# Attention masks of a recurrent four-layer network added by matmuls of 64 rows by 64 columns

## The chip, the cores and the metric

The program runs on one core of one Trainium2 chip. The metric is the device time of one execution in microseconds (us). The kernel before has a median of 2973.53 us over three runs. Engines are named as in the profile: PE is TensorE's matmul, PEld its weight load, DVE VectorE, ACT ScalarE, POOL GpSimd, and SPq the queue of SyncE, which issues the DMAs.

## The reference, cut to what matters

Four layers run one after another on 16 sequences ("rows") of 256 tokens and 128 channels. Each layer computes `x = x + s * silu(g)` from the layer norm `xn` of `x`. What matters here is the attention inside them:

```
L0 ffn:  local attention, twice (DEPTH = 2), 8 heads of 64, window 64:
         sim = q @ k^T;  mask = (i < j) | (i > j + 64);  softmax;  @ v
L1 attn: 16 heads of 8, causal, alibi bias;  softmax(att + bias) @ v
L2 attn: 16 heads of 8, causal, rotary, low-rank q, k, v
L3 attn: 16 heads of 8 + 32 rotary, causal, latent k, v
```

The other halves of the layers (a recurrent mixer, feed-forward networks, a mixture of experts, a Fourier filter) are not touched.

## The kernel before, in words

Each attention is one block in which every engine walks through a software pipeline of rows: in step `i` a row is projected, row `i-2` gets its scores and maxima, row `i-3` its exponentials, row `i-4` its values, row `i-5` its output (`rows_pipeline`, with a loop over the middle rows). Inside a step, rounds `x` go over pairs of heads, head e = 0 in rows 0 to 63 of the stacked operands and head e = 1 in rows 64 to 127. There are 4 rounds a row in the local attention (`local_attention`, called for two layers) and 8 in `attention`, which the alibi, the rope8 and the latent attention share. So there are 128 rounds in the local attentions together and 128 in each of the other three.

The scores are made twice. First, `scores` (L1156, local L731) writes q by k of a pair into two PSUM banks, one for each head, `masks` (L1163, local `score_masks`, L736 and L738) adds the mask, and DVE takes the row maxima (L1286 and L1287, local L921 and L922). Later the same scores are made transposed with the maximum subtracted by extra rows: `keyed` (L1175, local L749 and L754) writes into banks 6 and 7, `keyed_masks` (L1181, local L759 and L761) adds the mask, ACT takes the exponential (L1247, local L859), and `values` (L1196, local L774 to L776) multiplies by v. All of these matmuls accumulate into the same banks without clearing them after the first.

A mask is added by a matmul whose weights are the whole 128x128 identity and whose moving operand is a bf16 table: 128 columns of `causal_q` or `causal_k` for each of the two diagonal blocks of a head, or 128 and 192 columns of the local bands for a head. That makes four matmuls for a pair of heads and eight for a round, since the keyed masks and the score masks of a round follow each other. The last of each four signals ACT or DVE.

PE's order in a round of `attention` is: scores(x); keyed and keyed masks of an earlier row; score masks(x); then one of the odd jobs by x (x=0 `turn_back` L1134, x=1 `shifts` L1102, x=2 `output` L1141, x=5 `value_rows` L1114, x=7 `turn` L1125, and the projections `product`: one at x=3 in alibi, two at x=3 and 4 in rope8, five at x=2 to 6 in latent); in even rounds `values` of two pairs. In the local attention it is: scores; keyed; both masks; `columns_of` L718 (four transposes); `product` L709; value projection L782 or turn L794; values; at a row's end `output` L802.

What orders the rounds: `scores` waits until DVE has read the maxima of the bank that it reuses (`deep` is 2 bank pairs in alibi and rope8, 1 in the latent attention), `keyed` waits for the exponential of the round before (one bank pair), `keyed` at x=4 waits for a DMA of the row maxima (L1034), and `scores` at x=0 waits for the stacks of its row, brought by 18 DMAs a row in alibi and rope8 (L1046), which SPq issues behind that one. SPq in turn waits for `at_mt`, DVE's L1292 after `shifts`.

The tables come from `const_cast`, are loaded as f32 into `k.Y` by one DMA (L2136) and cast to bf16 by one DVE instruction (L2155) ahead of the first layer norm.

Of the kernel before, what the change touches and what calls it, by code (L numbers as in the profile page):

```python
# [19 lines left out]
P = 128  # L20
# [18 lines left out]
def const_cast():  # L39

    i = np.arange(P)
    ident = np.eye(P)
    causal = np.where(i[None, :] <= i[:, None], 0.0, BIG)
    band = lambda q, k: np.where((q - k >= 0) & (q - k <= 64), 0.0, BIG)
    q, k, j = i[:, None], i[None, :], np.arange(192)[None, :]
    local_q0 = band(q, k)
    local_q1 = band(q + 128, j + 64)
    local_k0 = band(j, i[:, None])
    sel = np.zeros((P, H8 // 2, P))
    for r in range(0, P, 32):  # L50
        for y in range(H8 // 2):
            sel[r + y, y] = 1.0
    parts = [("ident", ident), ("causal_q", causal), ("causal_k", causal.T), ("local_q0", local_q0),
             ("local_q1", local_q1), ("local_k0", local_k0), ("sel", sel.reshape(P, -1))]
    return parts


def const_f32():
# [76 lines left out]


CAST = widths([(n, a.shape[1]) for n, a in const_cast()])
CONF = widths([(n, a.shape[1]) for n, a in const_f32()])
DH = [d * 1 + h * D8 for d in range(D8) for h in range(H16)]
# [33 lines left out]

class Core:
    pass


def at_least(eng, sem, value):
# [448 lines left out]
def local_attention(k, layer, w, rope, X0, Yd):  # L627

    nc, s, ps = k.nc, k.s, k.ps
# [4 lines left out]
    with ExitStack() as ctx:  # L634
# [66 lines left out]
        def _(pe):  # L701
# [30 lines left out]
                                         start=(cols == 0), stop=False, skip_group_check=True)  # L732

            def score_masks():
                for e in range(2):
                    nc.tensor.matmul(ps[:, 4 + e, 0:P], k.cb("ident"), k.cb("local_q0"), start=False, stop=False,  # L736
                                     skip_group_check=True)
                    m = nc.tensor.matmul(ps[:, 4 + e, P:P + 192], k.cb("ident"), k.cb("local_q1"), start=False, stop=True,  # L738
                                         skip_group_check=True)
                m.then_inc(s.la_score, 1)  # L740

            def keyed(i, n, y):
                if y == 0:
# [11 lines left out]
                                         start=False, stop=False, skip_group_check=True)  # L755

            def keyed_masks():
                for e in range(2):
                    nc.tensor.matmul(ps[:, 6 + e, 0:P], k.cb("ident"), k.cb("local_k0", 0, P), start=False, stop=False,  # L759
                                     skip_group_check=True)  # L760
                    m = nc.tensor.matmul(ps[:, 6 + e, P:P + 192], k.cb("ident"), k.cb("local_k0"), start=False, stop=True,  # L761
                                         skip_group_check=True)
                m.then_inc(s.la_keyed, 1)

            def values(i, n, y):
                u = HP8 * (row0 + i) + y
# [47 lines left out]
            def step(i, n):  # L814
                for x in range(4):
                    row2, row3 = 2 + (x < 1), 3 + (x < 2)
                    if live(i, row2):
                        scores(i - row2, (n - row2) % NS, (x - 1) % 4)
                    if live(i, row3):
                        keyed(i - row3, (n - row3) % NS, (x - 2) % 4)  # L820
                        keyed_masks()
                    if live(i, row2):
                        score_masks()
                    row1 = 1 + (x < 1)
                    if live(i, row1):
                        if x == 1:
                            at_least(pe, s.la_stored, row0 + done(i, 5))
                        if x == 2:
                            at_least(pe, s.la_mt, row0 + done(i, 3))
                        columns_of(i - row1, (x - 1) % 4)  # L830
                    if live(i, 0):
                        product(i, n, x)
                    if live(i, 2) and x in (0, 2):
                        project_values(i, (n - 2) % NS, x // 2)
                    if live(i, 4) and x in (1, 3):
                        turn(i, x // 2)
                    row = 3 + (x < 3)
                    if live(i, row):
                        values(i - row, (n - row) % NS, (x - 3) % 4)
                    if live(i, 5) and x == 0:  # L840
                        output(i)
                    if live(i, 3) and x == 1:
                        shifts(i)
# [141 lines left out]
def attention(k, call, scale, stack_rows, rounds, product_at, value_from, value_w, out_w, out_b, make):  # L985

    nc, s, ps = k.nc, k.s, k.ps
# [3 lines left out]
    with ExitStack() as ctx:  # L991
        sb = lambda n, shape, dt=F32: ctx.enter_context(nc.sbuf_tensor(f"at{call}_{n}", shape, dt))
        a = Core()
# [5 lines left out]
        deep = 2 if split else 1  # L999
# [78 lines left out]
        def _(pe):  # L1078
# [78 lines left out]
                                         start=(cols == 0), stop=False, skip_group_check=True)  # L1157

            def masks(i, n, x):
                for e in range(2):  # L1160
                    o = ps[:, 2 + 2 * (x % deep) + e, :]
                    for cols in (0, 2 * P):
                        m = nc.tensor.matmul(o[:, cols:cols + P], k.cb("ident"), k.cb("causal_q"), start=False,  # L1163
                                             stop=(cols > 0), skip_group_check=True)
                m.then_inc(s.at_score, 1)

            def keyed(i, n, x):
                u = HP * (row0 + i) + x
# [7 lines left out]
                                         start=(cols == 0), stop=False, skip_group_check=True)  # L1176

            def keyed_masks():
                for e in range(2):
                    for cols in (0, 2 * P):  # L1180
                        m = nc.tensor.matmul(ps[:, 6 + e, cols:cols + P], k.cb("ident"), k.cb("causal_k"), start=False,  # L1181
                                             stop=(cols > 0), skip_group_check=True)
                m.then_inc(s.at_keyed, 1)

            def values(i, n, x):
                u = HP * (row0 + i) + x
# [14 lines left out]
            def step(i, n):  # L1201
                for x in range(HP):
                    if live(i, 2):
                        scores(i - 2, (n - 2) % slots, x)
                    row = 3 + (x < KEY_LAG)
                    if live(i, row):
                        keyed(i - row, (n - row) % slots, (x - KEY_LAG) % HP)
                        keyed_masks()
                    if live(i, 2):
                        masks(i - 2, (n - 2) % slots, x)  # L1210
                    if live(i, 5) and x == 0:
                        turn_back(i)
                    if live(i, 3) and x == 1:
                        shifts(i, n)
                    if live(i, 5) and x == 2:
                        output(i)
                    if live(i, 0) and x in product_at:
                        product(i, n, product_at[x])
                    if live(i, VALUE_ROW) and x == 5:
                        value_rows(i, (n - VALUE_ROW) % slots)  # L1220
                    if live(i, 4) and x == 7:
                        turn(i)
                    if x % 2 == 0:
                        row = 3 + (x < VALUE_LAG)
                        if live(i, row):
                            values(i - row, (n - row) % slots, (x - VALUE_LAG) % HP)
                            values(i - row, (n - row) % slots, (x + 1 - VALUE_LAG) % HP)
# [1105 lines left out]
```

## Time and profile before

| | us |
|---|---|
| median of three runs (2969.06 to 2974.83) | 2973.53 |
| the profiled execution's own time | 2965.65 |
| its span | 2963.8 |
| PE busy in it | 2372.4 (80%) |
| DVE busy | 1467.8 (50%) |
| ACT busy | 1140.7 (38%) |
| POOL busy | 637.5 (22%) |

The local attentions take most of the span from about 210 to 650 us and from 770 to 1210 us, the alibi attention 1370 to 1660, rope8 1965 to 2265 and latent 2440 to 2940. A matmul's duration in the profile is its time through the array, not the time that it keeps the next one waiting: read the distance from one start to the next for that. Rows of a timeline merge neighbours of one line: start, time from the first start to the last end, and their count. The start of the last of them is the start plus that time less the mean of one.

### The profile page before, as it was taken

Reading aid. Unit: us, or ns where it says so; the run is one execution under the profiler, and the core shown is the slowest. Engines: PE = TensorE matmul, PEld = TensorE weight load, DVE = VectorE, ACT = ScalarE, POOL = GpSimd, SP = SyncE. Lnnn points to the kernel's source line nnn. Section 1 sums busy time; section 2 is a strip of 40 time slices with the busy share of each in tenths; the row PEclk is TensorE's granted clock in tenths of the full one; section 3 lists DMA queues with packets and bytes.
Section 4 is the critical chain, followed back from the end, with each engine's and each line's share of the span. In section 5 each row is a group of like instructions: output and inputs, shape, how many; then the busy total and the mean of one; then the engine's idle time right before and its main releaser. Section 6 shows DMA issues by size and latency. Waiting matters only on the chain. (4 is left out here: it accounts for less than half of the span.)

```text
span 2963.8 us, 54617 instructions
## 1 busy us (share of the span) xinstructions
PE 2372.4 (80%) x19643; PEld 1552.7 (52%) x19644; DVE 1467.8 (50%) x3082; ACT 1140.7 (38%) x1810; POOL 637.5 (22%) x689
## 2 busy tenths in 40 slices
PE   5487999997799999785888458259997768999987
PEld 1133777773267777332555235135553315777764
DVE  4635666635466664445666123166663254554542
ACT  5623554523254444333555212225453421222223
POOL 0204443300344441011100320521110121211100
PEclk8797999998799999887999789579998867999997
DMA  2000000000000000002222311112220013332320
GB/s 106 0 0 1 1 1 0 0 1 0 0 1 1 0 0 1 1 4 61 76 71 61 144 47 35 46 54 67 72 69 2 32 39 96 99 91 91 91 73 29
DMA packets 81244, 115.93 MB, mean 39 GB/s; under 512 B 10352, under 2 KB 67184, under 8 KB 77720
## 3 DMA queue, kind: packets, MB, share of 16 engines
q1 hardware_dynamic: 79024, 109.35, 12.0%
q0 software_dynamic: 2048, 4.20, 0.5%
q8 instruction: 118, 1.93, 0.3%
q14 instruction: 54, 0.44, 0.0%
HBM read 69.57 MB, written 42.86 MB: 38 GB/s over the span
## 5 line engine op out<-in xcount | busy, mean ns | idle before, releaser
L1247 ACT ACTIVATE at_pr<-ps 128x768 f32<-128x768 f32 x384 | 312.1, 813 | 549.6 <-PE ps L1181 549.6
L1286 DVE TENSOR_REDUCE at_m<-ps 128x2 f32<-128x256 f32 x384 | 163.3, 425 | 424.8 <-PE ps L1163 417.7
L1156 PE MATMUL ps<-at_ks,at_qs 40*128 40x128 f32 (+5 forms) x2048 | 213.6, 308 | 79.4 <-DVE at_m L1287 38.4
L1287 DVE TENSOR_REDUCE at_m<-ps 128x2 f32<-128x512 f32 x384 | 262.1, 682 | 0.0
L692 POOL TENSOR_TENSOR la_tc<-la_ta,la_tb 128x512 f32<-128x512 f32 x128 | 162.3, 1268 | 356.7 <-DVE la_tb L958 356.7
L1175 PE MATMUL ps<-at_qs,at_ks 41*128 41x256 f32 (+5 forms) x2048 | 198.9, 293 | 41.0 <-DMA at_qs<-at_ml 24.1
L709 PE MATMUL ps<-w_l0f,la_hs 128*128 128x512 f32 x256 | 153.8, 686 | 54.9 <-POOL la_hs L674 37.0
L859 ACT ACTIVATE la_pr<-ps 128x640 f32<-128x640 f32 x128 | 90.3, 705 | 267.7 <-PE ps L761 267.4
L1175 PEld LDWEIGHTS ps<-at_qs,at_ks 41*128 41x128 f32 (+2 forms) x2048 | 142.7, 145 | 84.6 <-ACT at_pr L1247 33.5
L1156 PEld LDWEIGHTS ps<-at_ks,at_qs 40*128 40x128 f32 (+2 forms) x2048 | 100.4, 145 | 164.3 <-DVE at_m L1287 66.1
L1196 PE MATMUL ps<-at_pr,at_v 128*32 128x256 f32 (+1 forms) x3072 | 173.3, 337 | 10.5 <-issue 10.1
L956 DVE TENSOR_TENSOR la_ta<-ps,la_tab 128x512 f32<-128x512 f32 x128 | 88.5, 692 | 137.1 <-ACT la_sq L877 137.1
L1181 PE MATMUL ps<-cast 128*128 128x128 bf16 x1536 | 154.8, 224 | 0.0
L1533 POOL TENSOR_TENSOR at_parts<-at_ta,at_tb 128x512 f32<-128x512 f32 x64 | 81.1, 1268 | 341.8 <-DVE at_tb L1523 341.7
L1163 PE MATMUL ps<-cast 128*128 128x128 bf16 x1536 | 153.7, 224 | 0.0
L685 POOL TENSOR_TENSOR la_qn<-la_tc,la_rn 128x512 f32<-128x512 f32 x128 | 133.5, 1043 | 86.4 <-DVE la_rn L945 43.5
L1196 PEld LDWEIGHTS ps<-at_pr,at_v 128*32 128x32 f32 x3072 | 92.1, 110 | 83.5 <-issue 36.2
L1181 PEld LDWEIGHTS ps<-cast 128*128 128x128 bf16 x1536 | 87.9, 98 | 57.0 <-issue 42.5
L774 PE MATMUL ps<-la_v,la_pr 128*128 128x65 f32 x512 | 95.0, 267 | 21.4 <-DVE la_ot L913 21.4
L877 ACT ACTIVATE la_sq<-ps 128x512 f32<-128x512 f32 x128 | 76.7, 599 | 89.6 <-PE ps L709 89.6
L774 PEld LDWEIGHTS ps<-la_v,la_pr 128*128 128x128 f32 x512 | 80.3, 192 | 57.8 <-issue 47.1
L1163 PEld LDWEIGHTS ps<-cast 128*128 128x128 bf16 x1536 | 103.6, 100 | 11.5 <-issue 11.5
(309 smaller groups left out, 5009.7 us busy)
## 6 DMA issues: line engine op xcount, KB each, us to landing
scratch_latent<-at_parts SPq DMA_DIRECT2D x32, 640.0 KB, 4.3
at_qs<-scratch_latent SPq DMA_DIRECT2D x32, 320.0 KB
at_ks<-scratch_latent SPq DMA_DIRECT2D x32, 320.0 KB
scratch_alibi<-at_parts SPq DMA_DIRECT2D x32, 192.0 KB, 2.3
at_ks<-scratch_alibi SPq DMA_DIRECT2D x192, 32.0 KB
scratch_rope<-at_parts SPq DMA_DIRECT2D x32, 192.0 KB, 2.3
at_ks<-scratch_rope SPq DMA_DIRECT2D x192, 32.0 KB
moe_weights<-in_moe SPq DMA_DIRECT2D x1, 4096.0 KB
```

The costliest lines, as they stand in the source:

```text
L685: nc.gpsimd.tensor_tensor(heads(qn[:, x % 2, :]), heads(tc[:, x, :]), rn[:, x, :].unsqueeze(2).to_broadcast([P, H8, D64]), ALU.mult).then_ ...
L692: nc.gpsimd.tensor_tensor(tc[:, x, :], ta[:, x % 2, :], tb[:, x % 2, :], ALU.add).then_inc(s.la_tc, 1)
L709: nc.tensor.matmul(ps[:, 0, :], hs[:, n, t * P:(t + 1) * P], w("wq" if p < 2 else "wk"), start=True, stop=True).then_inc(s.la_product, 1)
L774: nc.tensor.matmul(ps[:, 3, o0:o0 + W65], p[:, P:2 * P], V[:, n, 0, h, :], start=True, stop=True)
L1156: nc.tensor.matmul(o[:, cols:cols + keys], q[:, block_q:block_q + P], kk[:, 0:keys], start=(cols == 0), stop=False, skip_group_check=True)
L1163: m = nc.tensor.matmul(o[:, cols:cols + P], k.cb("ident"), k.cb("causal_q"), start=False, stop=(cols > 0), skip_group_check=True)
L1175: nc.tensor.matmul(ps[:, 6 + e, cols:cols + L - first], kk[:, keys:keys + P], q[:, first:L], start=(cols == 0), stop=False, skip_group_che ...
L1181: m = nc.tensor.matmul(ps[:, 6 + e, cols:cols + P], k.cb("ident"), k.cb("causal_k"), start=False, stop=(cols > 0), skip_group_check=True)
L1196: m = nc.tensor.matmul(o, V[:, n, q, 4 * half + j, 24 * slot:24 * slot + 32], pr[:, x % RING, e, cols:cols + L - first], start=(q == 0 and ...
L1247: nc.scalar.activation(pr[:, p % RING, :, :], ps[:, 6:8, 0:384], ACT.Exp, scale=scale).then_inc(s.at_prob, 1)
L1286: nc.vector.tensor_reduce(m2[:, r, 0, x:16:8], ps[:, m:m + 2, 0:128], AX.X, ALU.max, negate=True)
L1287: nc.vector.tensor_reduce(m2[:, r, 1, x:16:8], ps[:, m:m + 2, 128:384], AX.X, ALU.max, negate=True).then_inc(s.at_max, 1)
```

## The change

The eight whole-array mask matmuls of a round become eight of 64 rows by 64 columns, four for the scores and four for the keyed scores. Each has a 64x64 piece of the identity as weights and moves half of a mask's rows. For head e the two matmuls read table rows 64e to 64e+63: one writes the same half of the partitions, and the other the opposite half, for which a second copy of each table is kept with its halves swapped (`_x`). Each moves all columns of its head at once: 2 x 128 (a stepped output) in `attention`, 320 in the local one. The local tables are joined to 320 columns. The packed constants grow from 1408 to 2432 columns, so the DMA L2136 and the cast L2155 do. The order of the work and all waits stay.

```
-    parts = [("ident", ident), ("causal_q", causal), ("causal_k", causal.T), ("local_q0", local_q0),
-             ("local_q1", local_q1), ("local_k0", local_k0), ("sel", sel.reshape(P, -1))]
-    return parts
+    masks = [("causal_q", causal), ("causal_k", causal.T), ("local_q", np.concatenate([local_q0, local_q1], 1)),
+             ("local_k", np.concatenate([local_k0[:, 0:P], local_k0], 1))]
+    crossed = [(name + "_x", np.roll(a, P // 2, 0)) for name, a in masks]
+    return [("ident", ident)] + masks + crossed + [("sel", sel.reshape(P, -1))]
...
+def mask_pair(k, bank, name, cols, twice=None):
+
+    half = P // 2
+    for crossed in range(2):
+        for e in range(2):
+            r = half * e
+            to = half - r if crossed else r
+            rows = k.cb(name + "_x" if crossed else name)[r:r + half, :]
+            out = k.ps[to:to + half, bank + e, 0:cols]
+            if twice:
+                out = out.rearrange("p (c t) -> p c t", t=P)[:, 0:cols // P:twice, :]
+                rows = rows.unsqueeze(1).to_broadcast([half, out.shape[1], P])
+            m = k.nc.tensor.matmul(out, k.cb("ident", r, half)[r:r + half, :], rows, start=False, stop=True,
+                                   skip_group_check=True)
+    return m
...
             def score_masks():
-                for e in range(2):
-                    nc.tensor.matmul(ps[:, 4 + e, 0:P], k.cb("ident"), k.cb("local_q0"), start=False, stop=False,
-                                     skip_group_check=True)
-                    m = nc.tensor.matmul(ps[:, 4 + e, P:P + 192], k.cb("ident"), k.cb("local_q1"), start=False, stop=True,
-                                         skip_group_check=True)
-                m.then_inc(s.la_score, 1)
+                mask_pair(k, 4, "local_q", 320).then_inc(s.la_score, 1)
...
             def keyed_masks():
-                for e in range(2):
...
+                mask_pair(k, 6, "local_k", 320).then_inc(s.la_keyed, 1)
...
             def masks(i, n, x):
-                for e in range(2):
-                    o = ps[:, 2 + 2 * (x % deep) + e, :]
-                    for cols in (0, 2 * P):
-                        m = nc.tensor.matmul(o[:, cols:cols + P], k.cb("ident"), k.cb("causal_q"), start=False,
-                                             stop=(cols > 0), skip_group_check=True)
-                m.then_inc(s.at_score, 1)
+                mask_pair(k, 2 + 2 * (x % deep), "causal_q", 384, 2).then_inc(s.at_score, 1)
...
             def keyed_masks():
-                for e in range(2):
...
+                mask_pair(k, 6, "causal_k", 384, 2).then_inc(s.at_keyed, 1)
```

## Rows read from the trace of the kernel before

**Rows 1.** Page, part 2: PE's granted clock in 40 slices, in tenths.

```profile
PEclk8797999998799999887999789579998867999997
```

**Rows 2.** Waits of PE, 210 to 660 us, local attention: total us, times, longest.

```profile
PE ps L709 <- POOL la_hs L674: 18.6, 15, 4.5
PE ps L774 <- DVE la_ot L913: 10.7, 14, 2.2
```

**Rows 3.** Waits of PE, 1380 to 1650 us, alibi attention.

```profile
PE ps L1175 <- DMA at_qs<-at_ml: 11.6, 16, 2.4
PE ps L1156 <- DMA at_ks<-scratch_alibi: 5.7, 11, 1.2
```

**Rows 4.** Waits of PE, 1975 to 2255 us, rope8 attention.

```profile
PE ps L1134 <- DVE at_ot L1310: 5.8, 14, 0.7
```

**Rows 5.** Waits of PE, 2455 to 2935 us, latent attention.

```profile
PE ps L1156 <- DVE at_m L1287: 32.4, 54, 1.2
```

**Rows 6.** Timeline of PE, alibi: start, us, engine, line, operation, count.

```profile
1501.57 0.87 PE L1196 MATMUL ps<-at_pr,at_v 128*32 128x256 f32 x16
...
1502.81 0.40 PE L1181 MATMUL ps<-cast 128*128 128x128 bf16 x4
1503.04 0.39 PE L1163 MATMUL ps<-cast 128*128 128x128 bf16 x4
1503.27 0.39 PE L1102 MATMUL ps<-conf,at_m 128*128 128x128 f32 x2
1503.59 0.34 PE L1156 MATMUL ps<-at_ks,at_qs 54*128 54x128 bf16 x4
```

**Rows 7.** Timeline of PE, a local round: first mask, first transpose.

```profile
504.18 0.23 PE L759 MATMUL ps<-cast 128*128 128x128 bf16 x1
...
504.75 0.60 PE L718 MATMUL ps<-conf,la_qn 128*128 128x128 f32 x4
```

**Rows 8.** Groups of PE by form: mean ns of one is the last number.

```profile
L1163 PE MATMUL ps<-cast 128*128 128x128 bf16 x1536 | 153.7, 224 | 0.0
L1156 PE MATMUL ps<-at_ks,at_qs 54*128 54x256 bf16 x256 | 35.7, 275 | 0.0
```

**Rows 9.** Groups of weight loads by form.

```profile
L1181 PEld LDWEIGHTS ps<-cast 128*128 128x128 bf16 x1536 | 87.9, 98 | 57.0 <-issue 42.5
L1196 PEld LDWEIGHTS ps<-at_pr,at_v 128*32 128x32 f32 x3072 | 92.1, 110 | 83.5 <-issue 36.2 <-ACT at_pr L1247 16.9
L718 PEld LDWEIGHTS ps<-conf,la_qn 128*128 128x128 f32 x512 | 59.0, 146 | 15.6 <-issue 15.6
L731 PEld LDWEIGHTS ps<-la_qk 64*128 64x128 f32 x1024 | 67.3, 187 | 30.5 <-issue 21.4 <-DVE la_nm L922 5.0
```

**Rows 10.** Timeline of PE between 502.9 and 503.0 us, local scores.

```profile
502.69 0.49 PE L731 MATMUL ps<-la_qk 64*128 64x128 f32 x4
```

**Rows 11.** Timeline, a local row's first round: PE, ACT and DVE.

```profile
514.84 0.23 PE L759 MATMUL ps<-cast 128*128 128x128 bf16 x1
519.01 0.41 PE L774 MATMUL ps<-la_v,la_pr 128*128 128x65 f32 x2 [0.58 <-DVE la_ot L913]
515.32 0.70 ACT L859 ACTIVATE la_pr<-ps 128x640 f32<-128x640 f32 x1 [2.47 <-PE ps L761]
```

**Rows 12.** Timeline of SPq, alibi: first of the maxima, last of the stacks.

```profile
1505.06 1.36 SPq L1034 DMA_DIRECT2D at_qs<-at_mh  x2
...
1512.47 1.99 SPq L1046 DMA_DIRECT2D at_ks<-scratch_alibi  x6
```

**Rows 13.** Timeline, a latent round: PE and DVE.

```profile
2658.29 0.40 PE L1181 MATMUL ps<-cast 128*128 128x128 bf16 x4
...
2660.02 0.49 PE L1156 MATMUL ps<-at_ks,at_qs 40*128 40x128 f32 x4 [0.20 <-DVE at_m L1287]
2658.95 0.43 DVE L1286 TENSOR_REDUCE at_m<-ps 128x2 f32<-128x256 f32 x1 [3.05 <-PE ps L1163]
```

**Rows 14.** Timeline of DVE at the start: the cast of the tables.

```profile
12.76 0.89 DVE L2155 CAST cast<-y 128x1408 bf16<-128x1408 f32 x1 [11.84 <-DMA y<-in_cast]
```

More of the change, by code:

```diff
@@ L757, in keyed_masks @@
             def keyed_masks():
-                for e in range(2):
[L759 to L763, printed above, removed]
+                mask_pair(k, 6, "local_k", 320).then_inc(s.la_keyed, 1)
             def values(i, n, y):
@@ L1178, in keyed_masks @@
             def keyed_masks():
-                for e in range(2):
[L1180 to L1183, printed above, removed]
+                mask_pair(k, 6, "causal_k", 384, 2).then_inc(s.at_keyed, 1)
             def values(i, n, x):
```

## The prediction

> **What bounds the kernel now.** I read the granted clock first: in the slices that hold the middle of the attentions it is 9 or more tenths of full speed [rows 1], so their matmuls are priced at the 2.4 GHz level. Then I read the waits of PE in each attention, and then its timeline, start to start.
>
> In the local attention PE waits once or twice a row, at the row's first round, for POOL's shifted input and for DVE's division [rows 2]; the other three rounds run without a gap. In alibi it waits 16 times for the DMA of the maxima and 11 times for that of the stacks [rows 3]. These hang together: SPq issues from 1505.06 to 1514.46 us without a pause [rows 12], and scores(0) come only after that. So an alibi row is a fixed 11 us chain of DMAs behind `shifts`, plus the two rounds before it. In rope8 scores(0) do not wait for stacks. There PE waits for DVE's division ahead of `turn_back` [rows 4], which comes behind the maxima of round 7. In the latent attention, with one pair of score banks, scores wait for the maxima of the round before, 54 times in 128 [rows 5].
>
> **The mask block.** Before, eight matmuls take 1502.81 to 1503.27 = 0.46 us in the three attentions [rows 6], and 504.18 to 504.75 = 0.57 in the local one [rows 7]. The step of one of 128 columns is 0.056 (L1181's last starts at 1502.81+0.40-0.22 [rows 6, 8], L1163 at 1503.04).
>
> After, each four lie in four different tiles of the array. No row shows 64x64 tiles, so I bound them. The near row is `values`: 16 matmuls of 32 columns of weights, eight of 256 f32 columns and eight of 128, whose passes in series would take 8 x 0.21 + 8 x 0.105 = 2.5 us (0.105 from L1102's two in 0.39 and L718's four in 0.60). Their starts span only 0.87-0.28 = 0.59 [rows 6]: four tiles stream side by side, though all use the same rows. `scores` show the same for two row halves: four f32 passes in two steps [rows 10]. So I take four at a time: a group costs 2 x 0.055 = 0.11, or 0.135 with 320 columns, plus 0.02 for the staggered starts. The far bound is two at a time, 0.22 and 0.27 (first rival).
>
> The weight load of 64 bf16 columns lies between the 98 ns row of the whole identity and the 146 ns one of a transpose [rows 9]. Only the first of a block is uncovered, for 0 to 0.05 us more than now: 0.02. So a block becomes 2 x 0.11 + 0.02 + 0.03 = 0.27 us, and 0.32 locally: **0.19 and 0.25 less**.
>
> **The change of array shape.** L1102's two passes end their stream at 1503.27 + 0.21 = 1503.48, and L1156, which uses half the rows, starts at 1503.59 [rows 6]: 0.10 for changing the shape. Now scores (64x128) change once, into the masks (128x128), and the transposes and projections behind the masks keep that shape. After, the masks are 64x64, so where work of 128x128 follows there is **one change more**. It also uncovers a weight load: the first two passes of L731 after a change lie 0.49-0.28 = 0.21 apart instead of 0.11 [rows 10], so 0.10 for a load of 187 ns, and in proportion 0.05 for what L718's 146 has above 98 [rows 9]. An f32 load of 192 ns is half covered by a mask today, so it loses 0.05 too. Sum: **0.15 us a round** where such work follows: all local rounds, six of eight in alibi, seven in rope8, eight in latent. Bounds: 0, if 64x128 to 64x64 needs no stop (second rival), and 0.20. Behind a round with `values` or scores next there is a change of shape today too: nothing.
>
> The Trainium skill speaks against this change here ("TensorEngine Tiling (Array Packing)", Key Properties and Restrictions): a change of tiling mode drains the engine, and column tiling gives up the fast weight load. The trace agrees with the first, at 0.10 us; the second is not shown, since no bf16 load of under 128 columns stands in it.
>
> **The sum, stage by stage.** A round that PE sets wins 0.19-0.15 = 0.04 (local 0.25-0.15 = 0.10). A round set by the chain to ACT wins in the first four only: they need 0.10+0.02 to stream and 0.275 through the array [rows 8] instead of 0.40, so 0.08 (local 0.10). A round set by DVE's maxima wins the whole block, 0.19, since its second change of shape lies beside DVE.
> - Local: three rounds x 0.09 (0.24 - 0.15, unrounded) + the first, which hangs on keyed masks (514.84), exponential (515.32), division, values (519.01) [rows 11]: 0.10. That is 0.37 a row x 32 rows = 12 us. The first round's score masks win nothing: POOL's input is late there.
> - Alibi: all that is won from x=2 to 7 ends in the wait for the DMAs. Round 0 wins 0.04 and some 0.3 that PE waited ahead of `turn_back`, since round 7 now comes earlier against the DMAs; round 1 wins 0.08. 0.42 x 14 rows = 6 us.
> - Rope8: round 7 0.19 (DVE, `turn_back`), round 1 0.08, 4 0.04, 5 0.08; rounds 2 and 3 end in the wait for the maxima's DMA, 6 in `values`' wait for ACT, 0 in that for DVE. 0.39 x 15 = 6 us. The stacks had some 0.5 us to spare.
> - Latent: the round shown is 3.25 us, of which masks to DVE 0.66 [rows 13], DVE 1.1. By the timeline four rounds of eight wait long enough to win 0.19, one wins 0.13, and three are set by PE: 0.04 each. 1.0 x 15.5 = 15.5 us.
> - Start: the cast is the last thing ahead of the first layer norm, and waits for its DMA [rows 14]. 1024 columns more: 0.89 x 1024/1408 = 0.65 us on DVE, and the DMA's 704 KB become 1216, at the start's some 400 GB/s of shared queues 1.3 to 2.5 us. Together 2.5 us lost.
>
> 12 + 6 + 6 + 15.5 - 2.5 = 37 us. The profiled execution of 2965.65 (span 2963.8 and 1.85 around it) would be 2928.7. The median lies 7.9 us above it: 2973.5 - 37 = **2936.5 us**.
>
> **Rivals.** *Two at a time (slower).* The two matmuls of a head read the same rows of the array, and the crossed one waits for the direct one. Blocks would then take 0.48 and 0.58, so the 0.15 of each change of shape stands without return. Local 96 rounds x 0.17 = 16 us, latent 48 PE-set rounds x 0.17 + the rest = 10, rope8 3.5, alibi 0.5, start 2.5: 33 slower, **3006 us**. It decides from where the second two start over 0.06 us behind the first two (halfway between a sum of -37 and +33). For it: no row has tiles with shared rows and crossed columns and different row halves at once. Against it: `values`, four tiles on the same rows. The Trainium skill has a rule that would bring this about ("TensorE: Matmul & The Clock Gate", Part 3): a weight load overlaps running matmuls only when its row group differs. By that rule the crossed loads wait for the direct matmuls. The trace disagrees for column tiles, where 16 loads and matmuls span 0.59 us.
>
> *No stop between the two row-tiled shapes (faster).* Each block then starts 0.10 earlier: local 12 more, latent 12, rope8 6, alibi 2.5: 32 more, **2904 us**. For it: the row halves stay. Against it: every other change of columns or rows costs 0.10.
>
> *The waits take it all (no change).* If alibi and rope8 win nothing, the local PE-set rounds nothing (a change of shape at 0.20 and a load at 0.05), and the latent DVE rounds half: 2973.5 + 2.5 - 8 = **2968 us**.
>
> *The clock.* With less in the array, PE's clock could fall to 1.2 GHz in places. 23 of 40 slices are at 9 tenths or more [rows 1], 1704 us; if a twentieth of these, 85 us, ran at half clock with PE streaming two thirds of the time, as the timeline of the alibi rows has it, that costs 85 x 2/3 = 57 us: 2936.5 + 57 = 2993.
>
> **Chances.** Forecast 0.66, two at a time 0.14, no stop 0.10, all taken 0.07, clock 0.03. The forecast's own range is 2915 to 2962, by the bounds of the change of shape and the loads. For 8 in 10 I add the faster rival and leave the slower ones out: 2903 to 2965. About 0.2% is what a measurement of this kernel tells from no change. Faster 0.77 (forecast, no stop, and a little less), same 0.06, slower 0.17.
>
> **What the profile after would show.** Four mask matmuls starting within 0.03 us, the next four 0.11 later, and the block at 0.27 (right) or 0.48 (two at a time). A stop of 0.10 ahead of the first mask and again ahead of L718, L1102 or L1499; without the first, the second rival. In alibi longer waits for both DMAs; in the latent attention rounds of 3.06 instead of 3.25 us. The cast ending near 16 instead of 13.65. The prediction is wrong if the stops around small tiles cost more than 0.20, or if the latent rounds keep their length.

## The result, and the profile after

The change makes the kernel slower: 2985.72 us median of 20 runs (2965.93 to 3000.75) against 2964.91 of 20 runs of the kernel before, a ratio of 1.0068 with a 95% interval of 1.0050 to 1.0087. The forecast was 37 us faster, 2936.5 in a range that ended at 2965. Of the kernel before, three runs had stood at 2973.53 and twenty stand at 2964.91, so 8.6 us of the forecast's 2936.5 were in its base. The profiled execution of the changed kernel is the slowest of its twenty, 3000.75 us (span 2998.9): it shows 35 us of loss where the medians have 21. Ratios compare executions in the fast state; of all those below only one, of the wide masks, was not (3014.97 us).

Nearly every step about the matmuls came out as forecast. A local round of the changed kernel, on PE (start, us, engine, line; L191 is the matmul of `mask_pair`, L767 is what was L754, L736 what was L718), then a window of 0.03 us at the first four, and the weight loads of all eight:

```profile
505.41 0.31 PE L767 MATMUL ps<-la_mt,cast 64*128 64x128 bf16 x4
505.64 0.47 PE L191 MATMUL ps<-cast 64*64 64x320 bf16 x8
506.04 0.65 PE L736 MATMUL ps<-conf,la_qn 128*128 128x128 f32 x4
...
505.64 0.33 PE L191 MATMUL ps<-cast 64*64 64x320 bf16 x4
...
505.64 0.14 PEld L191 LDWEIGHTS ps<-cast 64*64 64x64 bf16 x8
```

The first four mask matmuls lie within 0.33 us from the first start to the last end, and one alone takes 0.309 in the mean, so they start within some 0.02 us: four tiles stream side by side, the crossed ones too. The eight end their stream 0.30 us after the first start (0.47 less 0.30 for the time that the last one's record takes, plus 0.133 for its 320 columns). Then comes a stop of 0.10 until L736. Block and stop together are 0.40 where they were 0.57 [rows 7].

An alibi round and a latent round of the changed kernel, PE and DVE:

```profile
1487.48 0.33 PE L1178 MATMUL ps<-at_qs,at_ks 56*128 56x256 bf16 x4
1487.74 0.41 PE L191 MATMUL ps<-cast 64*64 64x256 bf16 x8
1488.08 0.70 PE L1395 MATMUL ps<-xn,w_l 128*128 x2
...
2659.02 0.82 PE L1178 MATMUL ps<-at_qs,at_ks 41*128 41x256 f32 x8
2659.78 0.41 PE L191 MATMUL ps<-cast 64*64 64x256 bf16 x8
2660.12 0.70 PE L1149 MATMUL ps<-at_oT,w_l 128*128 128x256 f32 x2
```

From the first mask to the next whole-array matmul it is 0.34 us, of which 0.25 is the block and 0.09 the stop; it was 0.46 [rows 6]. The weight-load row (PEld) below tells what a 64-column bf16 load is: 108 ns, between the 98 and the 146 of [rows 9]. The two PE rows are the mask matmuls.

```profile
L191 PEld LDWEIGHTS ps<-cast 64*64 64x64 bf16 x4096 | 80.7, 108 | 97.4 <-issue 69.5
L191 PE MATMUL ps<-cast 64*64 64x256 bf16 x3072 | 181.6, 305 | 0.0
L191 PE MATMUL ps<-cast 64*64 64x320 bf16 x1024 | 61.6, 309 | 0.0
```

What did not come out is the clock. The page's row of the granted clock, after, against [rows 1], and the busy times with the granted clock (the number behind POOL) in the stretch of the latent attention, before and after:

```profile
PEclk8797999999799999877998697679988656997965
...
2440.00:2945.00 505.00, 452.81 (x4611) 337.98 (x4610) 224.01 (x480) 135.62 (x207) 79.21 (x75) 0.93 0.27 81
...
2425.00:2998.00 573.00, 524.03 (x4635) 347.82 (x4634) 238.75 (x500) 142.83 (x216) 80.30 (x76) 0.79 0.25 76
```

The last nine slices, which hold the latent attention, are 6, 5, 6, 9, 9, 7, 9, 6, 5 where they were 8, 6, 7, 9, 9, 9, 9, 9, 7. Since the clock has two levels, 1.2 and 2.4 GHz, a mean of 0.79 over 573 us means 2 x 0.21 x 573 = 241 us at the lower one; before it was 2 x 0.07 x 505 = 71. By the clock records of the two traces, from the first projection of a stage to its last output (us, and in brackets us at 1.2 GHz):

| stage | before | after | difference |
|---|---|---|---|
| local attention 1 | 440.8 (54.6) | 432.3 (50.0) | -8.5 |
| local attention 2 | 437.8 (48.5) | 430.6 (38.1) | -7.2 |
| alibi | 305.6 (35.9) | 306.8 (72.1) | +1.2 |
| rope8 | 319.5 (39.6) | 322.2 (79.9) | +2.7 |
| latent | 525.3 (81.8) | 574.7 (253.9) | +49.4 |
| all between, and the ends | 934.9 (341.9) | 932.2 (334.7) | -2.7 |

The rows of the latent attention show how the two go together. A row is the time from its first scores to the next row's (us, 15 of them, one execution):

```
before  24.9 31.2 28.2 28.6 28.7 28.6 29.9 28.7 28.6 29.9 30.0 28.6 28.7 28.7 26.2
after   30.7 37.2 38.6 27.5 27.6 27.5 29.0 29.0 27.5 29.1 40.9 27.5 27.6 27.6 30.7
```

At the high clock a row is 27.53 instead of 28.59 us, 1.06 shorter, as the forecast's 1.0 said. But the first three rows, the row behind the second turn of the loop and the last one run at the low clock. The loop holds the scores of rows 5 to 13. Of the 172 us more at the low clock, 65 lie ahead of it, 31 in it and 76 behind it. Most of the low clock behind it is one stretch, in which no turn of a loop lies:

```profile
2873.00:2941.00 68.00, 65.89 (x468) 42.89 (x468) 14.69 (x30) 15.11 (x23) 0.00 (x0) 0.50 0.07 19
```

One profile is one execution. But the record has the mean granted clock of each, and twice its distance from 1, times the span, is the time at 1.2 GHz. The twenty executions of the changed kernel have 788 us in the median (730 to 828, the profiled one at the top). The kernel before has 611 to 617 on the three chips of the experiments (579 to 657 over its 68 executions). So the change brings some 175 us more, not the 226 of the two profiles.

### The profile page after: what moved, and what is told of

Read it like the earlier page. It is cut to its first block and busy times, and to the rows that moved or that the text cites. A ratio compares the mean times of both kernels' runs of the same rounds, so it can differ in the third digit from the quotient of the medians.

```text
span 2998.9 us, 54617 instructions
## 1 busy us (share of the span) xinstructions
PE 2406.7 (80%) x19643; PEld 1446.5 (48%) x19644; DVE 1472.5 (49%) x3082; ACT 1141.1 (38%) x1810; POOL 636.5 (21%) x689
## 5 line engine op out<-in xcount | busy, mean ns | idle before, releaser
L1164 PE MATMUL ps<-at_ks,at_qs 40*128 40x128 f32 (+5 forms) x2048 | 237.4, 336 | 71.2 <-DVE at_m L1286 26.1
L1178 PE MATMUL ps<-at_qs,at_ks 41*128 41x256 f32 (+5 forms) x2048 | 220.7, 319 | 38.3 <-DMA at_qs<-at_ml 23.7
L191 PE MATMUL ps<-cast 64*64 64x256 bf16 (+1 forms) x4096 | 243.2, 306 | 0.0
L1195 PE MATMUL ps<-at_pr,at_v 128*32 128x256 f32 (+1 forms) x3072 | 191.6, 365 | 16.0 <-issue 15.5
L1178 PEld LDWEIGHTS ps<-at_qs,at_ks 41*128 41x128 f32 (+2 forms) x2048 | 158.3, 161 | 91.0 <-ACT at_pr L1246 31.6
L1164 PEld LDWEIGHTS ps<-at_ks,at_qs 40*128 40x128 f32 (+2 forms) x2048 | 111.9, 160 | 164.8 <-issue 70.6
L703 POOL TENSOR_TENSOR la_qn<-la_tc,la_rn 128x512 f32<-128x512 f32 x128 | 133.4, 1042 | 83.3 <-DVE la_rn L953 41.4
L191 PEld LDWEIGHTS ps<-cast 64*64 64x64 bf16 x4096 | 80.7, 108 | 97.4 <-issue 69.5
L782 PE MATMUL ps<-la_v,la_pr 128*128 128x65 f32 x512 | 95.0, 267 | 18.9 <-DVE la_ot L921 18.9
L782 PEld LDWEIGHTS ps<-la_v,la_pr 128*128 128x128 f32 x512 | 79.9, 191 | 56.4 <-issue 45.8
L749 PE MATMUL ps<-la_qk 64*128 64x128 f32 (+1 forms) x1024 | 105.7, 325 | 0.3 <-DVE la_nm L930 0.2
L783 PE MATMUL ps<-la_v,la_pr 128*128 128x65 f32 x512 | 99.0, 275 | 0.0
```

What stands on the lines that cost most here:

```text
L191: m = k.nc.tensor.matmul(out, k.cb("ident", r, half)[r:r + half, :], rows, start=False, stop=True, skip_group_check=True)
L703: nc.gpsimd.tensor_tensor(heads(qn[:, x % 2, :]), heads(tc[:, x, :]), rn[:, x, :].unsqueeze(2).to_broadcast([P, H8, D64]), ALU.mult).then_ ...
L749: nc.tensor.matmul(ps[:, 4 + e, cols:cols + hi - lo], q[:, first:first + P], kk[:, lo:hi], start=(cols == 0), stop=False, skip_group_check ...
L782: nc.tensor.matmul(ps[:, 3, o0:o0 + W65], p[:, P:2 * P], V[:, n, 0, h, :], start=True, stop=True)
L1164: nc.tensor.matmul(o[:, cols:cols + keys], q[:, block_q:block_q + P], kk[:, 0:keys], start=(cols == 0), stop=False, skip_group_check=True)
L1178: nc.tensor.matmul(ps[:, 6 + e, cols:cols + L - first], kk[:, keys:keys + P], q[:, first:L], start=(cols == 0), stop=False, skip_group_che ...
```

## The experiments

All of them carry the tables of the changed kernel, the wide masks wider ones; "whole" masks are the four 128x128 matmuls of the kernel before. Lengths and low-clock times are those of the profiled execution, ratios those of all runs against the kernel before on the same chip.

**Small masks in the local attentions alone.**

```
-                mask_pair(k, 2 + 2 * (x % deep), "causal_q", 384, 2).then_inc(s.at_score, 1)
+                mask_whole(k, 2 + 2 * (x % deep), "causal_q", CAUSAL_AT).then_inc(s.at_score, 1)
...
-                mask_pair(k, 6, "causal_k", 384, 2).then_inc(s.at_keyed, 1)
+                mask_whole(k, 6, "causal_k", CAUSAL_AT).then_inc(s.at_keyed, 1)
```

> Small masks in the two local attentions alone; whole-array masks elsewhere. Clock theory (the loss is PE's granted clock in the latent attention, the small masks themselves are quicker): the local attentions stay at 432 and 430 us as in the profile of the changed kernel, against 441 and 438, the latent one returns to 525, and the whole is 16 us faster than before, ratio 0.995. Rival (small masks cost time wherever they stand): no faster than before, ratio 1.000 or more.

Measured: 0.9954 (0.9932 to 0.9976), 2956.25 us against 2969.02. The local attentions took 432.4 and 430.7 us, the latent one 515.4 with 58.0 low. Small masks are quicker there, and the loss is not in them. The time at 1.2 GHz over all its runs is 612 us, 617 for the kernel before.

**Small masks in all but the latent attention.** `mask_pair` for calls 0 and 1 of `attention` and locally, `mask_whole` for call 2.

> Small masks in all but the latent attention. Clock theory: the local gain of 16 us less some 4 in alibi and rope8, where the changed kernel shows 36 and 40 us more at the low clock; latent at 525. Ratio 0.996. Rival (the low clock comes in the latent attention whatever its masks are, by chance or from what went before): latent at 570 to 580 us with some 250 at the low clock, ratio 1.007 as with the full change.

Measured: 0.9935 (0.9907 to 0.9964), 2950.77 us. Latent 514.0 us with 53.2 low, so the long low clock there does not come from small masks elsewhere. Alibi took 306.8 (75.5 low) and rope8 320.8 (72.6 low). This version beats both kernels.

**Small masks in the latent attention alone.** The opposite choice for each call.

> Small masks in the latent attention alone. Clock theory: latent attention 575 us with 254 at 1.2 GHz against 525 with 82, the whole 50 us slower, ratio 1.016. Rival (the clock falls there because of the stages before): latent 510 us at the high clock, ratio 0.995.

Measured: 1.0145 (1.0089 to 1.0201), 3011.86 us; the latent attention 564.7 us with 226.8 low, its first rows 30.7, 36.3 and 38.7. So the whole loss comes with the latent attention's own masks.

**Whole masks, half of them left out in the latent attention.** This separates how much PE streams from the shape in which it does. Head 0 of each pair stays unmasked, so the output is not the reference's.

```
-                mask_whole(k, 6, "causal_k", CAUSAL_AT).then_inc(s.at_keyed, 1)
+                mask_whole(k, 6, "causal_k", CAUSAL_AT, (1,) if call == 2 else (0, 1)).then_inc(s.at_keyed, 1)
```

> Whole-array masks everywhere, but in the latent attention only for the second head of each pair: half of the mask matmuls left out there, so that head 0 is not masked. The block streams 0.22 us, as long as the eight small ones, with no extra change of shape. Theory A (the clock falls because PE has less to stream in a round, whatever its shape): the latent attention shows much more than 82 us at the low clock, 150 or more, and is no shorter than 525 us. Theory B (it falls because of the 64x64 tiles or the extra stop): the clock stays as before, 80 us low, and the attention shortens by 20 to 30 us, to some 500.

Measured in the profile: the latent attention 537.2 us with 195.9 low, first rows 29.5, 35.2 and 37.9, loop rows 26.8. There is no small tile and no extra change of shape in this kernel, and the clock falls as with them: theory A's side. By all runs the ratio is 0.9967 (0.9932 to 1.0003), and there the fall is smaller than the profile shows: 675 us at 1.2 GHz in the median (617 to 740, the profiled one 713), 58 more than the kernel before, where small masks in the latent attention alone have 145 more. So less to stream lowers the clock without small tiles, but not in every execution. One difference is plain: this kernel's PE has no stop at the turns of the loop, and no low clock there.

**Small masks, each group issued twice in the latent attention.** The stream is as long as before, in the new shape.

```
             def keyed_masks():
+                if call == 2:
+                    mask_pair(k, 6, "causal_k", 384, 2)
```

> Whole-array masks elsewhere; in the latent attention the small masks, each group of four issued twice (the mask is added twice, which leaves the softmax as it is). PE then streams 0.45 us of masks in a round as before the change, in the small tiles and with the extra stop. Theory A (less to stream lets the clock fall): low clock in the latent attention back near the 55 to 82 us of the kernels with whole masks, rows of 28.7 to 29.5 us, the attention 520 to 535 us, ratio 1.00 to 1.005. Theory B (small tiles or the extra stop let it fall): over 200 us low, 580 us or more, ratio 1.02.

Measured: 1.0111 (1.0067 to 1.0156). The first rows are 25.5, 27.9 and 28.9 us, at the clock of the whole masks. But the attention took 556.8 us with 116.5 low, which neither theory had. The waits of PE show where the stops are (latent attention of this kernel, then of the changed one):

```profile
PE ps L1177 <- issue: 13.0, 4, 3.9
...
PE ps L1164 <- issue: 4.1, 2, 2.1
```

The loop has two turns, and at each PE stood still twice for 3.0 to 4.5 us from start to start, with nothing to wait for; in the changed kernel it is one stop of 2.3. Behind the two turns the clock was low for 34 and 31 us. So this run settles the first rows and not the loop. The longer body need not be what made the stops longer: the kernel with the groups twice only outside the loop (below) has the loop of the changed kernel, and stops as long:

```profile
PE ps L1164 <- issue: 12.1, 4, 3.4
```

**Small masks, wide instead of twice.** The same stream without more instructions: a table of 128 mask columns and 128 zeros, read twice.

```
-                mask_pair(k, 6, "causal_k", 384, 2)
+                mask_pair(k, 6, "causal_k", 512, 4)
...
+            if twice == 4:
+                out = out.rearrange("p (a t) -> p a t", a=2)
+                rows = rows.unsqueeze(1).to_broadcast([half, 2, 2 * P])
```

> Whole-array masks elsewhere; in the latent attention the small masks with a moving operand of 512 columns (the mask and zeros) instead of 256: as many instructions as the full change, the small tiles and the extra stop stay, and PE streams 0.43 us of masks in a round, as before the change. Theory A (less to stream lets the clock fall): the first three rows near 25, 28 and 29 us as with whole masks, loop rows 28.6 to 29.3, low clock under 100 us, the attention 520 to 535 us, ratio 1.000 to 1.004. Theory B (small tiles, extra stop): as with small masks in the latent attention alone, first rows 31, 36 and 39 us, 565 us, ratio 1.014. The loop turns stay short, which they were not where the groups were issued twice.

Measured: the latent attention 529.3 us with 65.0 low, first rows 25.5, 27.9 and 28.9, loop rows 29.2. This is theory A in both halves of its expectation on the clock. The ratio, 1.0055 (1.0023 to 1.0088), is above the 1.004 expected, and well below the 1.0145 of the small masks alone. The rows explain a part of it, 0.65 us x 15 = 10 us = 0.3%; the other 6 us are open, and they are not clock, with 608 us at 1.2 GHz in the median against 611. The clearest lines are those of one turn of the loop. First the timeline of PE in the changed kernel, then in this one:

```profile
2733.20 0.41 PE L191 MATMUL ps<-cast 64*64 64x256 bf16 x8
2733.55 0.65 PE L1133 MATMUL ps<-conf,at_raw 128*128 128x128 f32 x4
2736.27 0.71 PE L1164 MATMUL ps<-at_ks,at_qs 40*128 40x128 f32 x6 [2.07 <-issue]
...
2734.76 0.63 PE L195 MATMUL ps<-cast 64*64 64x512 bf16 x8
2735.32 0.66 PE L1150 MATMUL ps<-conf,at_raw 128*128 128x128 f32 x4
2738.03 0.93 PE L1181 MATMUL ps<-at_ks,at_qs 40*128 40x128 f32 x8 [2.06 <-issue]
```

The stop is the same, 2.07 and 2.06 us. What follows it, as busy times and granted clock of the stretches behind the stop, again the changed kernel first, then the wide masks, then the kernel before:

```profile
2737.00:2767.00 30.00, 29.49 (x186) 18.52 (x186) 8.24 (x17) 5.37 (x8) 1.85 (x2) 0.50 0.22 66
2770.00:2800.00 30.00, 28.62 (x319) 20.29 (x319) 16.01 (x35) 9.38 (x16) 6.45 (x6) 1.00 0.31 89
...
2740.00:2743.00 3.00, 3.00 (x30) 1.43 (x24) 1.02 (x2) 1.19 (x2) 0.00 (x0) 0.50 0.12 37
2743.20:2773.20 30.00, 28.63 (x300) 19.04 (x298) 14.62 (x31) 8.44 (x13) 5.40 (x5) 1.00 0.31 90
...
2734.00:2737.00 3.00, 3.00 (x26) 2.12 (x26) 0.80 (x2) 1.11 (x2) 0.00 (x0) 0.50 0.51 164
2738.00:2768.00 30.00, 28.16 (x311) 21.69 (x308) 14.57 (x31) 8.44 (x13) 5.40 (x5) 1.00 0.30 90
```

In all three the clock falls behind the stop. With 0.43 or 0.45 us of masks a round it is back after 3.4 us; with 0.22 it stays at 1.2 GHz for 30 us, in which PE issues 186 matmuls instead of 300 to 320. This is the clearest turn and not the rule. At its other turn the changed kernel, behind a stop of 2.04 us, is back after 3.4 us too:

```profile
2656.00:2686.00 30.00, 27.86 (x312) 19.46 (x310) 15.63 (x33) 9.48 (x15) 5.41 (x5) 1.00 0.28 90
```

Over all kernels whose turn has one stop, the low clock behind it lasts 0 to 6.8 us with the long stream (ten turns, 2.0 in the mean), and 0 to 30.7 with the short one (eight turns, 16.6 in the mean).

**Small masks, twice only outside the latent loop**, and **whole masks outside the latent loop**, the rest as in the changed kernel. Both try to keep the first rows at the high clock and the loop's rows short.

```
             def keyed_masks(i):
+                whole = call in (2,) and isinstance(i, int)
+                (mask_whole(k, 6, "causal_k", CAUSAL_AT) if whole else
+                 mask_pair(k, 6, "causal_k", 384, 2)).then_inc(s.at_keyed, 1)
```

> The full change, but in the steps of the latent attention that stand outside its loop (0 to 5 and 15 on) each group of small masks is issued twice. Theory A: the low clock of the first three rows goes (30.7, 37.2, 38.6 us in the changed kernel back towards 25, 28.3, 28.3), while the loop's rows keep 27.5 us; the attention takes 505 to 525 us and the whole is 0.7 to 1.2% faster than before. Theory B: no better than the changed kernel, 575 us. If the loop's own falls of the clock stay long, some 15 us are left on the table either way.

> The full change, but whole-array masks in the latent attention's steps outside its loop (0 to 5 and 15 on). Theory A: the first rows keep the high clock (25, 28, 28 us), the loop's rows take 27.5 instead of 28.6; the attention 500 to 515 us unless the clock falls at a turn of the loop and stays low for 30 us there, and the whole is 0.8 to 1.0% faster than before. If the loop's rows alone let the clock fall as the full change does: 540 us or more, ratio 1.000.

Measured: 1.0009 (0.9979 to 1.0040) with the groups twice, 0.9948 (0.9922 to 0.9975) with whole masks. Both regain much of the 1.0068. But the first rows did not come out clean: 32.4, 34.7, 28.9 and 30.3, 28.3, 38.1 us, so the stage started at the low clock in both executions. And in both a turn of the loop cost a long spell: 20 us low in the first, 31 in the second (row 11: 40.9 us). The latent attention took 538.7 (116.0 low) and 537.2 us (134.4 low), over the 505 to 525 and 500 to 515 expected, and neither ratio came near the 0.7 to 1.2% and 0.8 to 1.0% hoped for.

**Small masks in alibi and rope8 alone.**

> Small masks in the alibi and rope8 attentions alone. Clock theory: their loop rows are 0.4 us shorter (16.3 to 15.9, 17.3 to 16.9), and the first rows at the low clock give it back, so both attentions are within 3 us of before: ratio 0.998 to 1.001. Rival (the forecast's reckoning without the clock): 12 us faster, ratio 0.996.

Measured: 0.9994 (0.9972 to 1.0015). Alibi 304.3 us with 62.8 low, rope8 317.3 with 62.3 low: nothing won that can be measured, as the clock theory had it. Its latent attention has whole masks and yet 99.2 us low and 531.4 us in all, the most of the kernels with whole masks there.

**Small masks inside all three loops, whole ones outside.**

> The same in all three attentions: small masks in their loops and in the local attentions, whole ones outside the loops. Theory A: first rows of alibi and rope8 back near 10.5, 14.5 and 12.1, 14.8 us, loop rows 15.9 and 16.9, low clock of both at 36 to 50 us instead of 72 and 80; some 7 us faster than with whole masks outside the latent loop alone, ratio 0.987 to 0.990.

Measured: 0.9929 (0.9898 to 0.9961), 2948.3 us. Alibi 302.9 us (40.1 low) and rope8 320.5 (51.3 low), with first rows of 10.5, 14.2 and 12.1, 14.7: the low clock of their first rows goes with whole masks there. The latent attention took 526.6 with 110.2 low. The ratio is worse than the 0.987 to 0.990 expected, and its interval holds that of the version with whole masks in the whole latent attention, so the two aren't told apart.

**All kernels together.** The time at 1.2 GHz in the latent attention, from its first scores on, in the profile of each kernel (us). A star marks a part in which the masks of a round stream 0.22 us instead of 0.43 to 0.45. The last column is the time at 1.2 GHz of the whole program, the median of its runs less that of the kernel before on the same chip (to some 3 us, since the clock is recorded to three digits).

| kernel | rows 1 to 4 | loop, rows 5 to 13 | the rest | whole program |
|---|---|---|---|---|
| before | 35.3 | 3.4 | 23.9 | |
| small in local alone | 28.8 | 3.4 | 2.2 | -5 |
| small in all but latent | 29.2 | 3.4 | 2.1 | +37 |
| small in alibi and rope8 | 41.4 | 6.8 | 23.9 | +52 |
| small and wide in latent | 25.4 | 3.4 | 17.4 | -3 |
| small and twice in latent | 25.4 | 64.9 | 0.3 | +21 |
| twice outside the latent loop | 58.8 | 30.7* | 0.0 | +88 |
| whole outside the latent loop | 65.4 | 30.7* | 11.3 | +71 |
| small inside three loops | 35.0 | 30.7* | 18.0 | +14 |
| small in latent alone | 91.0* | 37.5* | 75.8* | +145 |
| whole, half left out | 88.7* | 0.0* | 79.8* | +58 |
| the changed kernel | 92.9* | 34.1* | 99.9* | +175 |

In the first and the last rows the starred parts lie above all others, whatever the shape. In the loop the stops at its turns count too: without them the short stream keeps the clock, and with 7 us of stops at each turn the long one loses it. Why two kernels with long masks in their first rows have 58.8 and 65.4 us there is open.

## Why the prediction was wrong

**The step that failed** is the clock. The prediction's first sentence priced all attentions at the 2.4 GHz level because the slices of the kernel before show it, and so a loss to the clock stood at nothing in the sum; the rival that doubted this got a chance of 0.03. In the profile 226 us more are at 1.2 GHz, 172 of them in the latent attention. With the clock of the kernel before, that attention would have taken 525 - 16 x 1.06 = 508 us; it took 575. So 172 us more at the low clock cost 67 us there, 0.39 us each; a line fitted through the twenty executions of the changed kernel gives 0.37. By all runs the 175 us more cost some 68 (an estimate, 175 x 0.39). The kernel is 21 us slower, so by the same estimate the matmuls and waits alone would have won some 47, and the forecast's 37 was not too much.

The rival had the mechanism. Its 85 us of work at the high clock would stretch by 57 to 142 us at the low one. Read so, it priced each us at the low clock at 0.40, which is right, and had 142 of them where some 175 came. Its 2993 us is the nearest of all the forecast's cases to what came, by some luck: a twentieth of the time was a guess without a stage, and its base and its other terms were off as well.

The experiments show the cause: in the latent attention the clock follows how much PE has to stream in a round. The small tiles and their stops, with the stream made long again, leave the clock as it was (65.0 us low there, and 608 us against 611 over all runs); whole masks with a short stream let it fall (195.9). That a short stream in small tiles costs no more than one in whole ones is not shown: over all runs it is 145 us against 58. The Trainium skill ("TensorE: Matmul & The Clock Gate", Part 1) has it that the throttled clock is the default and that activity releases it. The trace agrees as far as it goes: with the same tiles and the same stops, the attention is 65.0 us at 1.2 GHz with 0.43 us of masks a round, and 226.8 with 0.22.

**The mask block** was right: 0.25 us and 0.30 locally, where 0.27 and 0.32 were forecast, four tiles at a time. The rival of two at a time is out: the crossed tiles' weight loads do not wait for the direct tiles' matmuls. The rule of the Trainium skill that stood behind it ("TensorE: Matmul & The Clock Gate", Part 3) does not hold for these tiles: all eight loads lie within 0.14 us, where one takes 0.10, so the second four load while the first four stream.

**The change of shape** was right: a stop of 0.09 to 0.10 us ahead of the block and another behind it. The rival without a stop between the two row-tiled shapes is out: from the last start of L1178 (1487.48 + 0.33 - 0.21 = 1487.60) 0.05 us of stream go to 1487.65, and the mask starts at 1487.74.

**The local attentions** won 15.7 us, forecast 12, with 15 us less at the low clock, worth 6 us by the rate above. Two kernels with whole masks there (small in latent alone, and half left out) are within 2 us of the changed kernel's low clock; they are 5.4 us longer in each attention. So the masks gave some 10 to 11 us, and the 12 was right.

**Alibi and rope8.** Over six kernels with whole masks in their loops and six with small ones, the mean of the nine loop rows went from 16.55 to 16.24 us in alibi and from 17.34 to 17.06 in rope8: 0.3 less each, forecast 0.42 and 0.39. The wait for the stacks' DMA grew as it had to: 10.1 us in 12 waits of alibi, where it was 5.7 in 11 [rows 3]. The gain was given back in the first and last rows, where the low clock grew by 36 and 40 us: 12.1, 14.7 became 13.2, 16.8 us in rope8's first two rows.

```profile
PE ps L1164 <- DMA at_ks<-scratch_alibi: 10.1, 12, 1.6
```

**The latent attention's rows** were right at the high clock, 1.06 for 1.0, and wrong by all that the clock took.

**The start** cost less than forecast. The cast begins 0.8 us later and takes 1.43 instead of 0.89 [rows 14], so PE starts 1.34 us later instead of 2.5, and the first local attention starts at 221.3 us as before: what lies between took it up.

```profile
13.55 1.43 DVE L2154 CAST cast<-y 128x2432 bf16<-128x2432 f32 x1 [12.64 <-DMA y<-in_cast]
```

What stays open: why small masks bring a long low clock behind some turns of the latent loop, while the loops of alibi and rope8 have at most 3.4 us of it with either kind; no experiment was made on that.

## What to carry to other kernels

A stage at the full clock before an edit need not be there after it: when an edit takes streaming away from PE, look in the trace at the head and tail of its pipeline and at the turns of its loop, see how long the clock is low there, and price the stage at both levels. Take the clock of every execution, not of the profiled one alone. Make such an edit stage by stage and keep it where PE is still full: here the local attentions alone keep 0.5%. Small tiles that fill the array four at a time do halve a block of masks, at 0.10 us for each change of shape around them.

## What the runs showed of the hardware that was not expected

- At a turn of the latent loop two starts of PE lay 2.1 to 2.8 us apart with nothing to wait for. The clock was low behind that stop for 0 to 6.8 us with 0.43 to 0.45 us of masks a round, and for 0 to 30.7 us with 0.22.
- The stop at a turn is not fixed. It was two stops of 2.9 to 4.5 us in the two kernels with groups issued twice, in one of which the loop is that of the changed kernel, and there was none where half of the whole masks were left out. Why wasn't tested.
- Loading 64 bf16 columns as weights takes 108 ns in the mean, 10 more than 128 columns of the same type.
